# First column group of two tiles multiplied on each arriving piece of W, and one load of x issued earlier

## The reference

```python
att = softmax(gelu(gelu(emb @ W0 + b0) @ W1 + b1) @ W2 + b2)
agg_w, agg_b = einsum('bk,koi->boi', att, weight), att @ bias_k
h = einsum('boi,bih->boh', agg_w, x) + agg_b[:, :, None]
gate = softmax(h @ gate_W.T); the two largest, normalised -> w_dense
out = h @ W_base.T + einsum('ter,eor->to', (h . A) * w_dense * 2.0, B)
return x + out
```

## Time and profile before

| | |
|---|---|
| median of three runs | 258.31 us (257.84 to 259.67) |
| the profiled execution's own time | 258.37 us |
| its span, from first to last instruction | 256.7 us |
| PE busy, share of the span | 248.0 us, 97% |
| DVE, ACT, POOL busy | 49%, 30%, 17% |
| mean granted clock of PE | 0.987 of full |

### The profile page before, as it was taken

One profiled execution on the slowest core, in us unless ns is written; L12 is line 12 of the kernel. 1 busy time (PEld: TensorE's weight loads), 2 busy tenths in 40 slices (PEclk: granted clock), 3 DMA queues, 4 the chain that ended last, 5 costly groups with the idle time before them and its releaser, 6 DMA issues.

```text
span 256.7 us, 4234 instructions
## 1 busy us (share of the span) xinstructions
PE 248.0 (97%) x1451; PEld 243.2 (95%) x1451; DVE 127.0 (49%) x397; ACT 76.2 (30%) x169; POOL 43.4 (17%) x40
## 2 busy tenths in 40 slices
PE   7799999999699999999999999999999999999994
PEld 5699999999699999999999999999999999999993
DVE  2978635348464444446345434536344434535542
ACT  4558697111313141223122141213113121312110
POOL 3000245300303030401204040310304040120000
PEclk9689999999999999999999999999999999999999
DMA  6999964015160706033150705124060604212022
GB/s 201 403 399 326 408 239 154 12 71 204 43 245 0 245 3 232 15 116 129 45 200 0 245 1 188 57 84 161 0 245 0 225 20 142 106 71 93 0 84 82
DMA packets 10681, 35.25 MB, mean 137 GB/s; under 512 B 1200, under 2 KB 1712, under 8 KB 10672
## 3 DMA queue, kind: packets, MB, share of 16 engines
q1 hardware_dynamic: 10672, 35.12, 38.6%
HBM read 26.73 MB, written 8.39 MB: 137 GB/s over the span
## 4 chain that ended last, share of the span: by engine, by line
PE 90%; DMA 4%; DVE 3%; SPq 1%; ACT 1%; issue 1%; DVEq 0%; ACTq 0%
PE z_ps L700 25%; PE z_ps L701 24%; PE z_ps L702 24%; PE o_ps L719 3%; PE o_ps L714 3%; PE o_ps L716 3%; PE o_ps L730 3%; PE o_ps L728 3%; DMA w_raw<-wext_in 2%; DMA xt_raw<-xt_in 2%; DVE out_sb L562 1%; DVE blk_lo L491 1%; PE s_ps L744 1%; PE o_ps L808 1%; DVE z_lo L484 0%
## 5 line engine op out<-in xcount | busy, mean ns | idle before, releaser
L700 PE MATMUL z_ps<-w_hi,xt_hi 128*128 128x366 f32 (+1 forms) x384 | 129.4, 337 | 1.8 <-DVE w_lo L479 1.8
L701 PE MATMUL z_ps<-w_lo,xt_hi 128*128 128x366 f32 (+1 forms) x384 | 127.8, 333 | 0.0
L702 PE MATMUL z_ps<-w_hi,xt_lo 128*128 128x366 f32 (+1 forms) x384 | 127.5, 332 | 0.0
L700 PEld LDWEIGHTS z_ps<-w_hi,xt_hi 128*128 128x128 f32 x384 | 73.0, 190 | 2.8 <-issue 1.9
L484 DVE TENSOR_TENSOR z_lo<-z_ps,z_hi 128x366 fp32r<-128x366 f32 (+1 forms) x48 | 25.8, 538 | 98.9 <-ACT z_hi L354 98.9
L701 PEld LDWEIGHTS z_ps<-w_lo,xt_hi 128*128 128x128 f32 x384 | 73.3, 191 | 0.2 <-issue 0.2
L702 PEld LDWEIGHTS z_ps<-w_hi,xt_lo 128*128 128x128 f32 x384 | 73.0, 190 | 0.0
L317 POOL TENSOR_TENSOR xt_lo<-xt_raw,xt_hi 128x1024 fp32r<-128x1024 f32 x14 | 35.9, 2566 | 149.7 <-ACT xt_hi L344 149.7
L354 ACT ACTIVATE z_hi<-z_ps 128x366 fp32r<-128x366 f32 (+1 forms) x48 | 22.8, 475 | 128.0 <-PE z_ps L702 128.0
L558 DVE TENSOR_TENSOR out_sb<-o_ps,x_nat 128x366 f32<-128x366 f32 (+1 forms) x44 | 20.0, 507 | 4.2 <-PE o_ps L730 3.8
L344 ACT ACTIVATE xt_hi<-xt_raw 128x1024 fp32r<-128x1024 f32 x15 | 15.9, 1057 | 10.1 <-DMA xt_raw<-xt_in 10.1
(11 more groups left out here) (96 smaller groups left out, 159.5 us busy)
## 6 DMA issues: line engine op xcount, KB each, us to landing
x_nat<-x_in SPq DMA_DIRECT2D x16, 512.0 KB, 4.7
xt_raw<-xt_in SPq DMA_DIRECT2D x15, 512.0 KB, 5.4
out<-out_sb SPq DMA_DIRECT2D x15, 512.0 KB, 3.0
w_nat<-wn_in SPq DMA_DIRECT2D x8, 512.0 KB, 10.6
w_raw<-wext_in SPq DMA_DIRECT2D x8, 366.0 KB, 8.7
w_raw<-wext_in SPq DMA_DIRECT2D x4, 364.0 KB, 5.4
par<-small_in SPq DMA_DIRECT2D x1, 576.0 KB, 7.0
xt_raw<-xt_in SPq DMA_DIRECT2D x2, 256.0 KB, 3.7
```

The source lines that it names most:

```text
L700: nc.tensor.matmul(dst, hi, w_cols(w_hi, g, k), start=(k == 0), stop=False)
L701: nc.tensor.matmul(dst, hi, w_cols(w_lo, g, k), start=False, stop=False)
L702: last = nc.tensor.matmul(dst, lo, w_cols(w_hi, g, k), start=False, stop=(k == KC - 1))
```

## The change

Four things are changed in order, and nothing in what is computed.

1. x of tile 1 is loaded in two halves between the first W pieces, like that of tile 0; its high parts come from ACT in two halves, its low parts from DVE, both earlier in their queues. PE goes through tile 0's and tile 1's first column group side by side: for each piece of W first tile 0, then tile 1. Tile 0's first group goes to the bank `o_ps[0]`, so that tile 1's can have `z_ps[0]`; the aggregation takes `o_ps[1]`, `o_ps[2]`, `t_ps` and `z_ps[2]`. Tile 1's later groups follow where its first one stood, and its transpose moves into the next step.
2. The dummy matmuls after the small network go from one to four.
3. x of tile 2 is loaded ahead of the first natural-layout loads.
4. x of the fifth tile (t = 4) is loaded ahead of the stores behind the late bias, after a wait for POOL's low part of tile 2.

```diff
+        Z_FIRST = [(0, 0), (1, 0), (0, 1), (0, 2), (1, 1), (1, 2)]
+        agg_banks = [o_ps[1], o_ps[2], t_ps, z_ps[2]]
+        def z_at(t, g):
+            return o_ps[0] if isinstance(t, int) and (t, g) == (0, 0) else z_ps[g]
@@ sync
+            load_x01(0, 0)
+            load_w(0)
+            load_x01(1, 0)
+            load_w(1)
+            load_x01(0, 1)
+            load_x01(1, 1)
+            load_w(2)
+            load_w(3)
...
+            sp.wait_ge(x01_lo_ready, 3)
+            load_xt(2, 0)
             load_xn(0, 0)
             load_xn(1, 1)
...
+            sp.wait_ge(x_lo_ready, 1)
+            load_xt(4, 0)
             for t in range(2):
                 sp.wait_ge(late_biased, t + 1)
                 sp.dma_start(out_t[t], out_sb[:, t, :]).then_inc(out_stored[t], 16)
-            step(1, 1)
+            step(1, 1, load_t=False)
@@ scalar
+            x1_high(0)
             w_high(1)
...
+            x1_high(1)
+            for n in range(2, 2 * PER_G):
+                w_high(n)
...
             z_high(0, 2, first=True)
+            x_high(1, 0, first=True)
+            z_high(1, 0)
             row_sum(0)
-            row_sum(1)
...
-            x_high(1, 0)
             block_high(1, 1, first=True)
-            z_high(1, 0)
+            row_sum(1)
+            z_high(1, 1)
             row_sum(2)
             row_sum(3)
+            ratio_exp(1)
@@ vector
             w_low(0)
+            dve.wait_ge(x1_hi_ready, 1)
+            x_low(1, 0)
             dve.wait_ge(mlp_mm, 3)
             nc.vector.tensor_reduce(att_max[:, 0:1], s_ps[0:BATCH, 64:64 + K], AX.X, ALU.max,
                                     negate=True).then_inc(att_step, 1)
+            w_low(1)
             x0_high(1)
             x_low(0, 1)
-            w_low(1)
+            dve.wait_ge(x_hi_ready, 1)
+            x_low(1, 1)
             dve.wait_ge(att_exped, 1)
             nc.vector.reciprocal(att_inv[:, :], att_sum[:, :]).then_inc(att_step, 1)
@@ tensor
-            warm(1)
-            pe.wait_ge(x01_lo_ready, 1)
-            z_group(0, 0, 0, chunks=range(PC + 1), by_piece=True, bank_free=True)
+            warm(4)
+            def first_z(t, q):
+                pe.wait_ge(x01_lo_ready, 1 + t + 2 * (q // 2))
+                z_group(t, t, 0, chunks=range(PC * q, PC * (q + 1)), by_piece=True, bank_free=True)
+            first_z(0, 0)
+            first_z(1, 0)
+            first_z(0, 1)
             pe.wait_ge(att_step, 3)
...
+            first_z(1, 1)
+            first_z(0, 2)
+            first_z(1, 2)
+            first_z(0, 3)
             pe.wait_ge(att_step, 4)
...
+            first_z(1, 3)
             pe.wait_ge(diag_ready, 2)
...
-            z_group(1, 1, 0, chunks=range(KC - 2))
+            z_group(1, 1, 1, chunks=range(KC - 2))
...
             o_group(1, 1, 1)
-            transpose_lora(1)
```

More of the change, by code:

```diff
@@ L148, in build @@
         x0_loaded = [sem("x0_loaded_first"), sem("x0_loaded_second")]
+        x1_loaded = [sem("x1_loaded_first"), sem("x1_loaded_second")]
         xt_loaded = [sem("xt_loaded_even"), sem("xt_loaded_odd")]
@@ L185, in build @@
         x0_hi_ready = sem("x0_hi_ready")
+        x1_hi_ready = sem("x1_hi_ready")
         x01_lo_ready = sem("x01_lo_ready")
@@ L213, in x_half, with z_place @@
             return slice(half * D // 2, (half + 1) * D // 2)
+        def z_at(t, g):
+            return o_ps[0] if isinstance(t, int) and (t, g) == (0, 0) else z_ps[g]
+        def z_place(t, g):
+            if isinstance(t, int) and (t, g) in Z_FIRST:
+                return Z_FIRST.index((t, g)) + 1
+            return G * t + g + 1
         def z_cols(z, g):
@@ L229, in _, with load_x01, load_w @@
             sp.dma_start(par[:, 0:C_MLP], small[:, 0:C_MLP]).then_inc(mlp_loaded, 16)
[L230 to L233, removed]
+            def load_x01(t, half):
+                cols = x_half(half)
+                sp.dma_start(xt_raw[:, t, cols], xt[t][:, cols]).then_inc((x0_loaded, x1_loaded)[t][half], 16)
+            def load_w(n):
                 sp.dma_start(piece(w_raw, n), piece(wext, n)).then_inc(w_loaded[n], 16)
-                if n == PER_G - 1:
-                    sp.dma_start(par[:, C_MLP:C_ALL], small[:, C_MLP:C_ALL]).then_inc(par_loaded, 16)
-            load_xt(1, 1)
+            load_x01(0, 0)
[6 more added lines that the diff above has]
+            load_w(3)
+            sp.dma_start(par[:, C_MLP:C_ALL], small[:, C_MLP:C_ALL]).then_inc(par_loaded, 16)
+            for n in range(PER_G, PIECES):
+                load_w(n)
             for half in range(2):
                 sp.dma_start(out_sb[half * ER:(half + 1) * ER, 0, :], bt).then_inc(bt_loaded, 16)
+            sp.wait_ge(x01_lo_ready, 3)
+            load_xt(2, 0)
             load_xn(0, 0)
@@ L250, in _ @@
                 load_wn(n)
-            for t in range(2):
-                sp.wait_ge(x01_lo_ready, 2 * (t + 1))
-                load_xt(t + 2, t)
+            sp.wait_ge(x01_lo_ready, 4)
+            load_xt(3, 1)
             for n in range(NAT, KC):
@@ L338, in _, with x1_high @@
         def _(act):
+            def x1_high(half):
+                cols = x_half(half)
+                act.wait_ge(x1_loaded[half], 16)
+                nc.scalar.activation(xt_hi[:, 1, cols], xt_raw[:, 1, cols],
+                                     ACT.Copy).then_inc((x1_hi_ready, x_hi_ready)[half], 1)
             def x_high(j, parity, first=False):
                 t = 2 * j + parity
-                act.wait_ge(xt_loaded[parity], (j + parity) * 16)
-                if not first:
-                    act.wait_ge(z_done, G * (t - 1))
+                act.wait_ge(xt_loaded[parity], j * 16)
+                act.wait_ge(z_done, z_place(0, G - 1) if first else G * (t - 1))
                 nc.scalar.activation(xt_hi[:, parity, :], xt_raw[:, parity, :], ACT.Copy).then_inc(x_hi_ready, 1)
@@ L350, in z_high @@
             def z_high(t, g, first=False):
-                act.wait_ge(z_done, G * t + g + 1)
+                act.wait_ge(z_done, z_place(t, g))
                 if not first:
                     act.wait_ge(o_done, G * (t - 1) + g + 1)
-                nc.scalar.activation(z_cols(z_hi, g), z_ps[g][:, 0:WIDTH[g]], ACT.Copy).then_inc(z_hi_ready, 1)
+                nc.scalar.activation(z_cols(z_hi, g), z_at(t, g)[:, 0:WIDTH[g]], ACT.Copy).then_inc(z_hi_ready, 1)
             def block_high(t, parity, first=False):
@@ L427, in _ @@
             block_high(0, 0, first=True)
-            for n in range(2 * PER_G, PIECES):
+            for n in range(2 * PER_G + 1, PIECES):
                 w_high(n)
-                if n == 2 * PER_G + 2:
-                    z_high(0, 1, first=True)
+            z_high(0, 1, first=True)
             act.wait_ge(g_sum_mm, 1)
             nc.scalar.activation(w_sum[:, 0:GZ], s_ps[:, GS:GS + GZ], ACT.Copy).then_inc(g_sum_ready, 1)
-            x_high(0, 1, first=True)
             act.wait_ge(consts, 8)
@@ L627, in _ @@
                                     AX.X, ALU.add).then_inc(g_part_ready, 1)
-            w_low(PER_G)
+            for n in range(PER_G, 2 * PER_G):
+                w_low(n)
             dve.wait_ge(bias_mm, 1)
@@ L634, in _ @@
             z_low(0, 0)
-            for n in range(PER_G + 1, 2 * PER_G):
+            w_low(2 * PER_G)
+            block_low(0, 0)
+            for n in range(2 * PER_G + 1, PIECES):
                 w_low(n)
[L637 to L644, removed]
+            z_low(0, 1)
             dve.wait_ge(expert_ready, 1)
@@ L661, in _ @@
             z_low(0, 2)
+            z_low(1, 0)
             block_low(1, 1)
-            z_low(1, 0)
             dve.wait_ge(xn_loaded[0], 16)
@@ L750, in step @@
                 pe.wait_ge(x_lo_ready, t - 1)
-                z_group(t, parity, 0)
+                if sums:
+                    z_group(t, parity, 0, chunks=range(PC))
+                    transpose_lora(t - 1)
+                    z_group(t, parity, 0, chunks=range(PC, KC), bank_free=True)
+                else:
+                    z_group(t, parity, 0)
                 o_group(t - 1, 1 - parity, 2)
@@ L801, in _ @@
                              start=True, stop=True).then_inc(bias_mm, 1)
+            first_z(1, 3)
             pe.wait_ge(diag_ready, 2)
             for g in range(NG):
-                bank = (o_ps + [t_ps])[g // AGG_BANK]
                 at = g % AGG_BANK * OG * TILES
-                mm = nc.tensor.matmul(bank[:, at:at + OG * TILES], par[:, C_WL + P * g:C_WL + P * (g + 1)],
+                mm = nc.tensor.matmul(agg_banks[g // AGG_BANK][:, at:at + OG * TILES],
+                                      par[:, C_WL + P * g:C_WL + P * (g + 1)],
                                       att_diag[:, :, :].rearrange("p o t -> p (o t)"), start=True, stop=True)
@@ L817, in _ @@
             pe.wait_ge(agg_ready, NG // AGG_BANK)
+            pe.wait_ge(z_lo_ready, 1)
             o_group(0, 0, 0, bank_free=True)
@@ L820, in _ @@
```

(10 more changed lines are left out.)

18 lines of the change are left out of this document (4 added, 14 removed).

## The result

The changed kernel takes **256.40 us** (median of 7, 256.24 to 258.39) against 259.67 for the kernel before, run beside it: ratio 0.9899, 95% interval [0.9863, 0.9935]; the two medians alone would give 0.9874. The forecast of 255.7 against 258.31 was the same ratio, 0.9899. In microseconds the forecast lies 0.7 low: the kernel before, too, came out above the median of its first three runs each time that it was timed again (medians 258.9 to 259.7). The profiled execution took 256.4, its span is 254.7, 2.0 less than before.

What follows compares the result with a forecast made beforehand. PE was taken as the bound, paying where it idles, runs at its lower clock or loses work. Gains of 2.5 (tile 1's group) and 0.1 (fifth tile's x) make 2.6 off 258.4: 255.7 us, range 253.0 to 256.6.

Steps and rivals of the forecast that it cites:

- DVE sets its delay: Start: PE waits for DVE's att_rep, ending at 11.77; tile 0's second column group starts 1.6 us later, at 19.47.
- the dummies are worth nothing: Start: three more dummy matmuls fill PE's 1.36 us wait for the first w_low; cost nothing, at worst 0.1 us.
- The fifth tile's x (0.1): Near 60 us: early load removes a 2.42 us PE hole, POOL's split makes one of 2.35; gain 0.1 us.
- The rival, that DVE is first: Near 60 us: DVE's x_bias precedes POOL's split, the hole goes for good; 253.4 us, down to 253.1; chance 0.29.
- it priced the hole's going at 2.4: Near 60 to 70 us: PE's hole vanishing entirely would take 2.4 us off the time.
- Tile 1's first group (2.5): Start: 24 matmuls, 4.1 us, move into PE's waits for W; less a delay of 1.6, net gain 2.5 us.
- The condition that this piece still lands at 7.8: Start: W's second piece lands at 7.8 us as before, so w_low(1) keeps its start at 8.66.
- put the clock at 0.2 to 0.4: Start: if the clock falls at 8.1 and rises at 11.5, PE is 0.2 to 0.4 us worse.
- The rival of a clock at half to 14.95: Start: PE stays at half clock up to 14.95; 257.5 us with the hole, 255.2 without; chance 0.12.
- "Nothing" for the moved transpose and the banks: Same instructions in a busy stretch of the same engine: no effect on the time.
- The slower rival: Near 40 us: POOL's tile 2 low split comes too late for PE; slower by over 1% from 5.6 us late; chance 0.07.

Runs made afterwards that it cites:

- POOL's wait: Kernel before, with the fifth tile's x loaded early and POOL's split of it waiting for the fourth tile's block_low: 256.62 us, 0.9881.
- two different edits that leave only the collision harmless: Changed kernel with POOL's fifth-tile split behind the fourth tile's block_low: 253.91 us; or with the third tile's z_low ahead of the first x_bias: 253.87 us.
- old order: Kernel before, tile 1's group unmoved; in the table with early fifth-tile load and POOL's split held for block_low: one dummy 256.62 us, four 256.26.
- the square: Four kernels, all with early fifth-tile load and held POOL split: tile 1's group unmoved or moved, one or four dummies; 256.62, 256.26, 255.23, 253.91 us.
- new order: Changed kernel, tile 1's group moved; in the table with POOL's fifth-tile split held for block_low: one dummy 255.23 us, four 253.91 (timed twice).

## Why the prediction was right or wrong

Two steps failed, both in the start: that DVE sets its delay (a net of 2.5, where the profiles show 1.6), and that the dummies are worth nothing (they give 1.3 us). The part of the fifth tile's x held.

**The fifth tile's x (0.1): right, by its mechanism.** The load leaves the chain, and POOL's split takes its place: it gets on at the end of the late bias (59.27, by its end and its usual length), ahead of DVE's next instruction, and holds `x_bias`; PE's new hole is 2.18 where 2.35 was forecast, and the part gave 0.24. The rival, that DVE is first, is out: nowhere did an `x_bias` behind the late bias keep its 1.28 while a two-input split of POOL waited. Taken alone the load is worth nothing (1.0005), taken with POOL's wait 3.0, and two different edits that leave only the collision harmless give 2.8. What the prediction left out is the clock behind the hole: it priced the hole's going at 2.4, and it gave 2.8 and 3.0 (see the last section). The Trainium skill (GPSIMD Engine Reference, Key points) has GpSimd contend with VectorE instructions that have two SBUF inputs; the traces agree, 1.28 against 3.41, and `z_low`, with one such input, keeps 0.54. Here the instruction that waited got on between two instructions of the other engine.

**Tile 1's first group (2.5): "DVE sets that delay" failed.** It holds only when the clock is full from the first matmul: then PE waits 0.59 for `att_rep`, as forecast, and the second group starts at 19.86 (forecast 19.47; the rest is `att_rep`, late because the second piece of W is split at 9.18 and not at 8.66). The condition that this piece still lands at 7.8 did not hold: ACT waits for it up to 8.26 in the changed kernel. The profile before may have been an early one, since the other three of the old order split this piece at 8.96 to 9.31. In the changed kernel's own profile PE was at half level up to 10.9, came to `att_rep` 0.75 later than the forecast's 11.87, and the second group started 0.85 late: a net of 1.6. That this single pair of profiles gives 1.6 and not 2.5 has a second cause: the first piece of W was read at 6.62, not at 5.90. Other profiles of the old order read it at 6.02 to 6.43, of the new one at 6.32 to 6.76; whether the order of the loads or chance makes these tenths stays open.

**The dummies ("Cost nothing, at worst 0.1"): this step failed.** It asked what they cost and not what they bring, and put the clock at 0.2 to 0.4. Without the hole in the way the square reads:

| | one dummy | four |
|---|---|---|
| old order | 256.62, 0.9881 | 256.26, 0.9878 |
| new order | 255.23, 0.9843 | 253.91, 0.9794 and 0.9806 |

In the new order, both timed in one group, they give 1.3, which I had booked under the moved group; that group alone gives 1.4, and both together 2.7, the forecast's 2.5 by another sum. By the ratios these are 1.0, 1.0 and 1.9 to 2.3, where each ratio alone has an interval of 1 us or more to either side. The profiles point the same way: in the new order matmuls keep their full-level spacing from 8.6 to 12.3 us on with four dummies (eight profiles), from 12.6 and 14.5 on with one; in the old order from 10.5 on with four, from 12.0, 15.1 and 15.2 on with one. The rival of a clock at half to 14.95 did not come about with four dummies; with one it was half up to 12.4 in one profile and up to 14 in the other. The Trainium skill (TensorE: Matmul & The Clock Gate, What's actually happening) has the switch come at differing points from run to run; two executions of one kernel agree, one at full level from 8.3, one from 10.9.

**"Nothing" for the moved transpose and the banks: not shown wrong, but not tried; the moved row sums had no term in the sum.** In the old order's profiles the start with four dummies is 2.19 shorter and 1.79 of that is given back up to 42.5 us, to waits that the new order, with its row sum and transpose moved back and tile 1's group ahead, does not have: its profile has no idle row there. Which of these moves takes the waits away was not tried.

**The slower rival** (tile 2's low split) did not come: PE has no idle row near 40.

## What to carry to other kernels

Where a load ends a hole, ask which engine the load releases and what that engine shares with the one next in line: here a copy that came early put a two-input GpSimd instruction between two VectorE ones, and the cure was to let it wait, or to put what PE needs ahead of the collision; both beat the two kernels compared here (253.91 and 253.87 against 256.40 and 259.67). Cost filler matmuls by the level of the clock that the work behind them gets, not by the time that they fill. And an earlier start counts only as far as what comes next at its own time, here a row sum held by a DMA, can be moved behind it.

## What the runs showed of the hardware

- A GpSimd subtraction with two SBUF inputs (2.40 us) and a VectorE instruction with two did not run side by side: each was recorded longer by little less than what was left of the other (3.41 for 1.28, with 2.25 left; 3.20 for 2.40, with 0.95 left).
- After PE's idle of 2.0 to 2.3 us the clock fell in some executions (granted 0.54 and 0.67 in the 3.5-us stages shown) and in others not (1.00 from 62.5 to 71 us, before and after). A fall costs some 1.5 us: with the load put back, three executions at a mean granted clock of 1.000 took 256.01 to 256.31, five at 0.993 took 257.35 to 258.28, and the profile is of one of these five, with the clock below 1.00 only behind the hole (0.85 from 62.5 to 71). The kernel before shows the same two groups: of its 57 timings beside the experiments 27 are at 0.993, with a median of 260.5, and 30 at other values, with a median of 258.7. That these 27 are falls behind the hole is not shown, since its one profile, at 0.987, is not of that group. If they are, that is 0.8 on average, and would explain why taking away a hole of 2.2 to 2.4 gave 2.8 to 3.0.
- Up to 6.3 us PE has the same instructions in all fourteen profiles, and yet two dummies near 4.8 took 0.71 to 0.81 us in four of them (full level) and 1.20 in ten (half): the level at the start differs between executions by itself.
- The granted clock of a stage can mislead at the start. This stage of the changed kernel shows 1.00, though its matmuls start 0.31 apart up to 10.8:

```profile
8.10:11.50 3.40, 3.40 (x13) 3.27 (x13) 3.04 (x7) 2.57 (x6) 0.00 (x0) 1.00 1.04 416
```

The spacing of matmuls of one shape says which level it was.
